# First batch's preparation reordered, value rows of two tiles by one block-diagonal product, x kept turned in pairs of tiles, and norms from bf16, in an eight-batch graph-attention layer

## The reference

```python
feats   = einsum('bnf,hfo->bhno', h, kernel)
f_self  = einsum('bnf,hfd->hbnd', h, attention_kernel)
f_other = einsum('bnf,hfd->hbdn', h, attention_kernel_2)
scores  = einsum('hbnd,hbdm->hbnm', f_self, f_other)
masked  = a_h * scores
masked  = where(masked >= 0, masked, 0.2 * masked) / sqrt(16)
masked  = masked + where(a_h == 0, -1e9, 0)
attn    = softmax(masked, -1) * where(a_h == 0, 0, 1)
out     = relu(einsum('bhnm,bhmo->bhno', attn, feats) + bias)
x       = layernorm(x + out)
```

## Time and profile before

| | before |
|---|---|
| median of 3 runs | 963.24 us (962.54 to 963.36) |
| profiled execution, its own time | 963.38 us |
| its span, first to last instruction | 961.7 us |
| busy: TensorE, VectorE, ScalarE, GpSimd | 898.2, 807.9, 636.7, 339.3 us |
| mean granted TensorE clock | 0.995 |
| moved by DMA | 144.49 MB, mean 150 GB/s |

### The profile page before, as it was taken

The page is one execution under the profiler, slowest core; times in us unless marked ns, Lnnn a source line. Parts: engine busy times, 40 slices in busy tenths (PEclk is TensorE's granted clock), DMA queues, the critical chain, the costliest instruction groups (busy, mean ns, idle before and its releaser), DMA issues.

```text
span 961.7 us, 14256 instructions
## 1 busy us (share of the span) xinstructions
PE 898.2 (93%) x5048; PEld 281.5 (29%) x5048; DVE 807.9 (84%) x1515; ACT 636.7 (66%) x1249; POOL 339.3 (35%) x301
## 2 busy tenths in 40 slices
PE   5049999999999999999999999999999999999994
PEld 3013232232323332323322233232323223222231
DVE  4638878898899878998789988998789987899994
ACT  2027766776667766776667767677667766677773
POOL 5433072421832245520733217411545208212101
PEclk9999999999999999999999999999999999999997
DMA  5696749835797639937698448877499366972000
GB/s 179 99 264 147 191 87 222 212 70 144 135 232 194 151 81 166 252 101 190 105 254 185 90 134 137 230 176 191 68 206 215 79 184 113 244 186 63 17 1 16
DMA packets 197581, 144.49 MB, mean 150 GB/s; under 512 B 176288, under 2 KB 176288, under 8 KB 197504
## 3 DMA queue, kind: packets, MB, share of 16 engines
q1 hardware_dynamic: 197504, 143.53, 63.9%
HBM read 94.03 MB, written 12.51 MB: 111 GB/s over the span
## 4 chain that ended last, share of the span: by engine, by line
PE 90%; DVE 5%; DMA 2%; SPq 1%; issue 1%; ACT 0%; POOLq 0%; POOL 0%; DVEq 0%
PE z L471 54%; PE numer L495 28%; PE misc L419 3%; PE misc L425 2%; DVE z L729 2%; DVE part L652 2%; PE misc L455 1%; DMA parts_dram<-part 1%; PE misc L435 1%; SPq L206 1%; DMA maskT<-mask 1%; DMA bias_rep<-in_L_gnn_bias 0%; PE misc L413 0%; DVE norm L665 0%; DVE ob L751 0%
## 5 line engine op out<-in xcount | busy, mean ns | idle before, releaser
L729 DVE SCALAR_TENSOR_TENSOR z<-z,maskT 128x512 f32<-128x512 f32 (+1 forms) x1152 | 725.9, 680 | 128.2 <-PE z L471 99.4
L617 ACT ACTIVATE probs<-z 128x512 f32<-128x512 f32 (+1 forms) x1152 | 595.9, 593 | 286.1 <-PE z L471 284.8
L471 PE MATMUL z<-self_st,other_st 96*128 96x512 bf16 (+3 forms) x2304 | 562.9, 379 | 22.4 <-issue 13.9
L471 PEld LDWEIGHTS z<-self_st,other_st 96*128 96x128 bf16 (+1 forms) x2304 | 185.8, 98 | 488.7 <-ACT probs L617 306.7
L495 PE MATMUL numer<-probs,vals 128*32 128x512 f32 (+1 forms) x2304 | 301.1, 595 | 0.2 <-ACT probs L617 0.2
L318 POOL TENSOR_SCALAR mask<-edges 128x1500 int16<-128x1500 f32 x96 | 138.3, 1441 | 60.6 <-DMA maskT<-mask 43.1
L362 POOL TENSOR_TENSOR cent<-yb,mean 128x256 f32<-128x256 f32 x24 | 14.7, 612 | 320.0 <-DVE mean L764 320.0
L346 POOL TENSOR_SCALAR part<-proj 128x512 bf16<-128x512 f32 x21 | 13.0, 617 | 219.4 <-ACT proj L593 219.4
L495 PEld LDWEIGHTS numer<-probs,vals 128*32 128x32 f32 x2304 | 45.3, 108 | 118.2 <-ACT probs L617 95.1
L382 POOL MEMSET self_st<- 3x6144 bf16 x7 | 36.5, 5212 | 7.7 <-PE z L471 7.5
L419 PE MATMUL misc<-xT,w_proj 64*128 64x512 f32 x48 | 29.8, 703 | 2.9 <-DMA bias_rep<-in_L_gnn_bias 1.5
(11 more groups left out here) (54 smaller groups left out, 224.2 us busy)
## 6 DMA issues: line engine op xcount, KB each, us to landing
edges<-in_adj SPq DMA_DIRECT2D x88, 750.0 KB, 5.9
parts_dram<-part SPq DMA_DIRECT2D x24, 384.0 KB, 4.9
self_st<-parts_dram SPq DMA_DIRECT2D x48, 192.0 KB, 5.3
other_st<-parts_dram SPq DMA_DIRECT2D x48, 192.0 KB, 5.9
edges<-in_adj SPq DMA_DIRECT2D x8, 468.8 KB
x_sb<-in_x SPq DMA_DIRECT2D x8, 352.0 KB
out<-cent SPq DMA_DIRECT2D x8, 352.0 KB
maskT<-mask SPq DMA_TRANSPOSE x96, 6.4
```

The lines of the kernel that those rows point to most:

```text
L471: return nc.tensor.matmul(z[:, v % BUFS * STEP + i, 0:WIDTH[st]], other_st[par][rows, h, c * P:(c + 1) * P], self_st[par][rows, h, st * W: ...
L617: nc.scalar.activation(probs[:, g % PROBS, v % UNITS * STEP:(v % UNITS + 1) * STEP, 0:WIDTH[st]], z[:, v % BUFS * STEP:(v % BUFS + 1) * ST ...
L729: nc.vector.scalar_tensor_tensor(banks, banks, FLOOR, maskT[(par + st) % 2][:, c, 0:WIDTH[st]].unsqueeze(1).broadcast_to([P, STEP, WIDTH[s ...
```

## The change

- TensorE, steady rounds: x is kept turned as pairs of tiles on 128 rows (`xT` is [128, 6, 128]). Projections use weights in the upper or the lower 64 rows, the other half being zeros (`w_proj[:, 0 or 1]`), and the tiles' order inside a round follows `PROJ_TILES`. Value rows come from a block-diagonal `w_val` [128, 128]: 6 products of 128 columns in place of 12 of 64. The norms' products take bf16 squares in place of float32 ones.
- GpSimd's splits per batch: five steps of three in place of six; the third part is written as bf16 by the subtraction itself, and the splits start once all three projections are out.
- Batch 0: the weights go on ScalarE's queue, into both halves (6 loads, and the bias), before ScalarE's table load. TensorE first does 12 turns of the identity. x, the projections and the value rows go to banks of `z` and not through `misc`. ScalarE casts the first part straight from PSUM, issues the part writes and all stack loads, and makes the squares; VectorE subtracts from PSUM. SyncE issues the transposes as soon as masks are made, and the second adjacency loads wait for all stacks. GpSimd makes the rows of ones and zeros and `head_sum` ahead of the masks, as half as many float32 elements with the same bits; the second buffer's ones come in the first stage.

Diff, cut to its core:

```diff
+SPLITS = 5 * NS
+PROJ_TILES = (((0, 8, 0),), ((8, 12, 0), (1, 5, 256)), ((5, 12, 0),))
...
-            for k in range(3):
-                stack(0, k, 0, 0)
             for j in range(SJ):
                 sp.wait_ge(mask_made, j + 1)
                 turn(0, 0, j)
+
+            sp.wait_ge(stacks_in, 16 * STACK_DMAS)
+            for j in range(SJ):
                 load_edges(0, 1, j)
...
+            pool.memset(other_st[0][KR:KR + 3, :, :].bitcast(F32), ONES).then_inc(ones_rows, 1)
+            pool.wait_ge(ones_rows, 1)
+            pool.memset(self_st[0][KR:KR + 3, :, :].bitcast(F32), 0.0).then_inc(shift_rows, 1)
+            pool.wait_ge(shift_rows, 1)
...
+            for j in range(SJ):
+                pool.memset(mask[j][:, N:NPAD].bitcast(I16), NO_EDGE_BITS).then_inc(mask_pads, 1)
+            pool.wait_ge(mask_pads, SJ)
+            for j in range(SJ):
+                make_mask(0, 0, j)
...
+                    pool.tensor_tensor(parts[2][:, cols], rest[:, cols], parts[1][:, cols],
                                        ALU.subtract).then_inc(splits, 1)
...
+            def project(dst, r):
+                for t0, t1, c in PROJ_TILES[r]:
+                    n = (t1 - t0 + 1) // 2 * P
+                    m = nc.tensor.matmul(dst[:, c:c + n], w_proj[:, t0 % 2, :], xT[:, t0 // 2:t0 // 2 + n // P, :],
+                                         start=True, stop=True, skip_group_check=True)
+                return m
+
+            def value_rows(dst, r):
+                for c in range(4 * r, min(4 * r + 4, NT // 2)):
+                    m = nc.tensor.matmul(dst[:, (c - 4 * r) * P:(c - 4 * r + 1) * P], xT[:, c, :], w_val[:, :],
+                                         start=True, stop=True, skip_group_check=True)
+                return m
...
-                                             proj[:, k * W:(k + 1) * W], start=True, stop=True,
+                                             squares[:, k * W:(k + 1) * W], start=True, stop=True,
...
             pe.wait_ge(ident_ready, 1)
+            for k in range(WARM_UP):
+                nc.tensor.transpose(misc[:, 0:P], ident[:, :], ident[:, :])
             pe.wait_ge(x_in, 32)
+            for r in range(XT_ROUNDS):
+                turn_x(z[:, r, :], 0, r).then_inc(first_full, 1)
+            pe.wait_ge(weights_in, 96)
+            for r in range(NS):
+                pe.wait_ge(first_taken, XT_ROUNDS)
+                project(z[:, 2 + r, :], r).then_inc(first_full, 1)
+            for r in range(2):
+                value_rows(z[:, (5, 0)[r], :], r).then_inc(first_full, 1)
+            pe.wait_ge(consts, CONSTS)
+            pe.wait_ge(pads, 3)
+            for r in range(2):
+                norms_round(r, VALS_ROUNDS + r + 1, 0)
+            pe.wait_ge(first_taken, XT_ROUNDS + 2)
...
+
+            act.wait_ge(w_zeros, 2)
+            for k in range(2):
+                rows = slice(k * F, (k + 1) * F)
+                act.dma_start(w_proj[rows, k, 0:HF].rearrange("f (h d) -> f h d", h=H),
+                              w_self.rearrange("h f d -> f h d")).then_inc(weights_in, 16)
+                act.dma_start(w_proj[rows, k, HF:2 * HF].rearrange("f (h d) -> f h d", h=H),
+                              w_other.rearrange("h f d -> f h d")).then_inc(weights_in, 16)
+            for k in range(2):
+                act.dma_start(w_val[k * F:(k + 1) * F, k * HF:(k + 1) * HF].rearrange("f (h d) -> f h d", h=H),
+                              w_feat.rearrange("h f d -> f h d")).then_inc(weights_in, 16)
+            act.dma_start(bias_rep[:, :],
+                          bias.rearrange("a b h d -> (a b) (h d)").broadcast_to([P, HF])).then_inc(bias_in, 16)
...
+
+            for r in range(XT_ROUNDS):
+                act.wait_ge(first_full, r + 1)
+                take_xT(z[:, r, :], r).then_inc(first_taken, 1)
+            for r in range(NS):
+                act.wait_ge(first_full, XT_ROUNDS + r + 1)
+                take_proj(parts[0], z[:, 2 + r, :], r).then_inc(first_part[0], 1)
+            act.wait_ge(first_part[0], NS)
+            act.dma_start(parts_dram[0, :, :], parts[0][:, :]).then_inc(parts_out, 16)
+            for r in range(NS):
+
+                act.wait_ge(first_rest, r + 1)
+                nc.scalar.activation(squares[:, r * W:(r + 1) * W], z[:, 2 + r, 0:W], ACT.Square).then_inc(first_squares, 1)
+            act.wait_ge(vals_init, 4)
+            for r in range(2):
+                act.wait_ge(first_full, PROJ_ROUNDS + r + 1)
+                take_values(z[:, (5, 0)[r], :], 0, r).then_inc(first_taken, 1)
+            first_stack(0)
+            for k in (1, 2):
+                act.wait_ge(first_part[k], NS)
+                act.dma_start(parts_dram[k, :, :], parts[k][:, :]).then_inc(parts_out, 16)
+                first_stack(k)
...
+            for r in range(NS):
+                dve.wait_ge(first_part[0], r + 1)
+                for t0, t1, c in PROJ_TILES[r]:
+                    n = (t1 - t0 + 1) // 2 * P
+                    m = nc.vector.tensor_tensor(
+                        rest[:, :].rearrange("p (t n) -> p t n", n=P)[:, t0:t1:2, :],
+                        z[:, 2 + r, c:c + n].rearrange("p (t n) -> p t n", n=P),
+                        parts[0][:, :].rearrange("p (t n) -> p t n", n=P)[:, t0:t1:2, :], ALU.subtract)
+                m.then_inc(first_rest, 1)
+            for r in range(NS):
+                cols = slice(r * W, (r + 1) * W)
+                dve.wait_ge(first_rest, NS)
+                nc.vector.tensor_copy(parts[1][:, cols], rest[:, cols]).then_inc(first_part[1], 1)
+            for r in range(NS):
+                cols = slice(r * W, (r + 1) * W)
+                dve.wait_ge(first_part[1], r + 1)
+                nc.vector.tensor_tensor(parts[2][:, cols], rest[:, cols], parts[1][:, cols],
+                                        ALU.subtract).then_inc(first_part[2], 1)
+            dve.wait_ge(first_part[2], NS)
+            dve.sem_inc(splits, SPLITS)
```

More of the change, by code:

```diff
@@ L1 @@
+import struct
 from contextlib import ExitStack
@@ L41 @@
 FLOOR = 2.0 ** -40
+ONES = struct.unpack("f", struct.pack("I", 0x3F803F80))[0]
 SELF_PART = (0, 0, 1, 1, 0, 2)
@@ L50 @@
 NEWTON = NS + ROOT - 1
-SPLITS = 6 * NS
+WARM_UP = 12
+SPLITS = 5 * NS
 MAXIMA = NT * H
@@ L133, in gat_layer @@
         weights_in = sem("weights_in")
+        bias_in = sem("bias_in")
+        w_zeros = sem("w_zeros")
+        first_full = sem("first_full")
+        first_taken = sem("first_taken")
+        first_rest = sem("first_rest")
+        first_squares = sem("first_squares")
+        first_part = [sem(f"first_part{k}") for k in range(3)]
         x_in = sem("x_in")
@@ L209, in stack @@
             def stack(buf, k, done, written):
-                sp.wait_ge(splits, done + (NS, 4 * NS, 6 * NS)[k])
+                sp.wait_ge(splits, done + (NS, 4 * NS, 5 * NS)[k])
                 sp.dma_start(parts_dram[k, :, :], parts[k][:, :]).then_inc(parts_out, 16)
@@ L305, in _ @@
                                pattern=[[-1, P]], channel_multiplier=1).then_inc(ident_ready, 1)
-            for j in range(SJ):
-                pool.memset(mask[j][:, N:NPAD].bitcast(I16), NO_EDGE_BITS).then_inc(mask_pads, 1)
             def make_mask(b, st, j):
@@ L408, in _, with turn_x @@
         def _(pe):
-            def xT_round(buf, r, n):
-                pe.wait_ge(misc_free, n)
+            def turn_x(dst, buf, r):
                 for k in range(3):
                     j = 6 * r + 2 * k
-                    m = nc.tensor.transpose(misc[:, k * P:(k + 1) * P],
+                    m = nc.tensor.transpose(dst[:, k * P:(k + 1) * P],
                                             x_sb[buf][:, j:j + 2, :].rearrange("p j f -> p (j f)"), ident[:, :])
-                m.then_inc(misc_full, 1)
-            def proj_round(r, n):
-                pe.wait_ge(misc_free, n)
-                nc.tensor.matmul(misc[:, 0:W], w_proj[:, :], xT[:, r * W:(r + 1) * W],
-                                 start=True, stop=True).then_inc(misc_full, 1)
-            def vals_round(r, n):
-                pe.wait_ge(misc_free, n)
-                for c in range(8 * r, min(8 * r + 8, NT)):
-                    m = nc.tensor.matmul(misc[:, (c - 8 * r) * HF:(c - 8 * r + 1) * HF], xT[:, c * P:(c + 1) * P],
-                                         w_val[:, :], start=True, stop=True)
-                m.then_inc(misc_full, 1)
+                return m
[9 more added lines that the diff above has]
+                                         start=True, stop=True, skip_group_check=True)
+                return m
             def norms_round(r, n, split_done):
@@ L543, in batch @@
                 pe.wait_ge(shift_rows, b + 1)
-                pe.wait_ge(ones_rows, 2)
+                pe.wait_ge(ones_rows, 1 if first else 2)
                 for n in range(GB):
@@ L603, in numer_out, with first_stack @@
                 nc.scalar.copy(o_sb[:, :], numer[:, 0:W]).then_inc(numer_free, 1)
-            for r in range(VALS_ROUNDS):
```

(18 more changed lines are left out.)

124 lines of the change are left out of this document (48 added, 76 removed).

## The result

The changed kernel takes **928.7 us** (median of 4 runs, 927.9 to 929.6); the kernel before took 963.2 in the same session (4 runs). The ratio is 0.964 (95% interval 0.963 to 0.966), so it is faster by 34.5 us. The profiled execution took 928.04, its span is 926.2. The forecast was 934, its range 925 to 947.

What follows compares the result with a forecast made beforehand. The prediction took TensorE, busy 93% of the span, to bound the kernel. From 963.4 us it took 14.7 for the start and 14.0 over seven batches, giving 934.7, stated as 934; range 925 to 947.

Steps and rivals of the forecast that it cites:

- (b): Main loop, value rows: half the records, the doubled columns hidden beside the weight load; 1.35 us a batch.
- (c): Main loop, norms: bf16 squares take one pass in place of float32 products; 0.65 us a batch, passed on.
- (1): Start: the weights, on ScalarE's queue, land at 10 us, bounds 9.3 and 14.2.
- rival B: Start: part writes and stack loads share full DMA engines with transposes and adjacency; start gains 7, 942 us; chance 0.20.
- Step (2): Start: three projections at 2.08 us each end at 16.2, ScalarE's last cast at 16.8, no waits for copies between.
- The 0.7 for a lost head start of TensorE: Start: TensorE no longer has four scores ready, so its first values product loses about 0.7 us.
- step (4): Start: the casts' stall goes, second write issued at 22.7, not 36.37; behind six stack loads it lands at about 32.
- (a): Main loop, projections: the same 1536 columns in four products gain nothing, bounds -0.3 and +0.2.
- Rival D: TensorE's clock is up for the first projections, 3.1 us less, and rounds lose part of their 0.13; 929 us; chance 0.13.
- C: Rival, main loop: the value rows' doubled columns aren't hidden, giving 0 to 0.7; 939 to 944 us; chance 0.13.
- E: Rival, main loop: VectorE takes the norms' gain, its reduction late by as much; 4.5 us back, 938.5; chance 0.03.
- F: Rival: the flag falls, bf16 norms cross the limit and the slow branch runs 196 us; over 1120 us; chance 0.01.

Runs made afterwards that it cites:

- e4: The changed kernel with SyncE waiting for the six weight loads before it issues the adjacency loads: 933.72 us, ratio 0.970.
- e6: The changed kernel with batch 0's four mask transposes issued behind the wait for all stack loads: 936.99 us, ratio 0.973.
- e5: The changed kernel with GpSimd's constant rows filled as bf16 behind the masks again, which brings the casts' stall back: 929.18 us, ratio 0.966.
- b2: The kernel before with batch 0's mask transposes moved behind the first stack's loads, second adjacency loads behind all stacks: 953.44 us, ratio 0.991.
- b1: The kernel before with 64-row operands of projections and value rows filled up to 128 rows with zeros: 952.03 us, ratio 0.989.
- e2: The changed kernel with value rows in 12 products of 64 columns on 128 rows, not 6 of 128: 935.87 us, ratio 0.973.
- e3: The changed kernel with norms from float32 squares and float32 head_sum again: 931.44 us, ratio 0.968.
- e7: The changed kernel without the 12 turns of the identity: 929.37 us, ratio 0.965.
- e10: The changed kernel with the second and third part's writes issued by SyncE, stack loads left on ScalarE's queue: 923.75 us, ratio 0.959.
- best_writes_x: The changed kernel with SyncE issuing the second and third part's writes and batch 1's x loaded ahead of the second adjacency loads: 920.7 us.

## Why the prediction was right, and where it was wrong

The measured 928.7 lies in the range, and in part by luck. The loop gave 23.4 us where its upper bound was 17.5, and the start gave less than forecast. What bounds each part, the order of the start's links and the mechanisms of (b) and (c) were right; two terms were mis-sized.

**The start: right in its chain, 2.7 too much.** The step that was mis-sized is (1), the landing of the weights: 15.57, beyond even its bound of 14.2. I took 4.6 us from the earlier trace rows, where the loads stood ahead of the adjacency on one queue. On ScalarE's queue, beside adjacency loads on SyncE's, they took a median of 9.8 from issue to landing, and the sixth was issued at 5.9 and not at 5.2. That is rival B's mechanism, and e4 shows it by taking the neighbour away. The later steps carry the lateness on: last cast 21.2 (16.8 forecast), stack loads from 23.6 (20), second write 26.3 to 35.6 (22.7 to 32), third landed 44.6 (41), TensorE 50.7 (47.5). Their own lengths held: 9.2 us for the second write against 9.3, and 9.0 from there to the third against 9.0. Step (2) gave 1.2 back: four products took 4.99 where it had 3 x 2.08 = 6.24. In e4, where the clock is at its lower level through all four, they take 5.47; so about 0.8 comes from products that follow one another without a copy between, and 0.5 from the granted clock, which rose at 19.9, during the last of them. The 0.7 for a lost head start of TensorE did not come: its first values product starts 7.25 us behind the first mask step, against 7.70 before. The transposes are hidden, as said, and where the change puts them they do the stacks no harm (e6), which refutes B's other half.

**"Here the stall goes" in step (4) named a real wait, and its removal gained little.** The removal is worth at most 0.9 us (e5), since the six stack loads take the stall's place, as the same step said. What pays is that the transposes left the end of the queue: 9.0 by b2. The other 3 are the stacks, 3.5 earlier at TensorE.

**The main loop: the step that was mis-sized is (a), "the same 1536 columns in four products: nothing".** I counted columns and instructions and took no cost for the number of rows. For the three projections it is 0.56 a batch in the rounds and 0.3 in the scores behind them, 0.86 for a forecast of nothing. The value rounds pay it too, and b1 gives all five rounds by themselves: 10.3 us with nothing else changed. The "0.13 besides" that I took in (b) as a round's fixed price was most of that switch; without it a value round is just 8 records of 0.111, so (b) was 0.27 too small, and 0.2 more lies in the scores behind its two rounds. Rival D had this in half a sentence, "rounds that lose part of their 0.13", at 2 us over the run. The bound of -0.3 for (a) was too narrow for the rounds alone, which gave 0.56 a batch, and it left out the scores behind them, though their 0.76 was there to be read.

**(b)'s mechanism and (c) were right.** A record of 128 columns costs as much as one of 64 (e2), so C is out. The norms give 0.66 for a forecast 0.65, and all of it is passed on (e3), so E is out: TensorE's turn behind them waits as long for VectorE as before, 0.5 us.

**D** is out for the first projections. The granted clock did rise behind the turns, to its upper level from 6.3 to 9.7, but it fell while TensorE waited for the weights. The projections run at the lower level until the last of them, and the turns of the identity buy nothing that can be measured (e7). **F** did not happen. Not foreseen was the wait for x of batch 1; the forecast looked only at the masks behind the moved adjacency loads, and not at the load of x that stands behind them on the same queue. One reading was loose: the start is the first 7% of the trace, not the first hundredth.

**Left open:** whether e4 together with e10 would pay, whether the third part write's 9.7 us could be halved by fewer stack loads ahead of it, what the adjacency and the transposes each do to the writes in e4, and whether the second part's write would be as quick on ScalarE's queue if it were issued before the loads. None of it was tried.

## What to carry to other kernels

Price a product by its rows too: one with another number of rows than its neighbours can cost time before it and behind it, and the place to see that is the duration of the *following* group, compared with the same group elsewhere. When a load moves to another queue, ask what runs beside it on the shared DMA engines, what was issued before it on any queue, and what then stands behind it in its own; each can matter more than the load. When a stall is removed, look for what would have covered it: here the stall of 14 us was worth under 1, and four transposes in the wrong place were worth 9.

## What the runs showed of the hardware

- Filling 64-row float32 operands up to 128 rows with zeros made each round 0.2 us shorter and the three scores behind it 0.1 shorter (b1): 10.3 us of 962.4 for no work less.
- Six small loads (16 KB) on one queue took a median of 9.8 us to land beside 750 KB loads on another. With those held back (e4) the last, issued at 5.33, was in by 7.4.
- A 384 KB write issued behind six 192 KB loads landed after 9.2 us on their queue, and after 9.7 on another (best_writes_x). Issued ahead of five of them, on another queue, it took 4.2. The Trainium skill (Trainium Kernel Development and Optimization, Key Constraints) says that queues of several engines run on the same 16 DMA engines and interleave, and that issuing from several engines saves issue time alone. The trace of e10 agrees on issue time: 2.4 us sooner at issue brought the write in 7.4 sooner and the first mask step 6.5. It does not show the interleaving for the third write, of which no packet moved from 28.6 to 32.6.
- TensorE's granted clock fell to its lower level for 3.4 us behind waits of 2.2 us (e10), 2.1 (e4) and 1.7 (e7) in the main loop, and not behind the changed kernel's 0.89.
- GpSimd's fill of 3 rows costs by elements and not by bytes: 2.65 us for 3072 float32 a row, 5.38 for 6144 bf16, the same bytes.
